# Preparation of a graph kernel: root steps between statistics, index rows cast as they land, spare tile tables ahead of the index transposes

## What is computed

```python
def _layernorm(x, axis=-1, eps=1e-05):
    m = jnp.mean(x, axis=axis, keepdims=True)
    v = jnp.var(x, axis=axis, keepdims=True)
    return (x - m) / jnp.sqrt(v + eps)
...
def _gin_agg(h, src, dst, eps, n_nodes):
    agg = jax.ops.segment_sum(h[src], dst, num_segments=n_nodes)
    return (1.0 + eps) * h + agg
...
x = x + _L0_gnn_ref(_layernorm(x, axis=-1), edge_index, ...)
x = x + _L0_ffn_ref(_layernorm(x, axis=-1)[None], ...)[0]
x = x + _L1_gnn_ref(_layernorm(x, axis=-1), edge_index, ...)
x = x + _L1_ffn_ref(_layernorm(x, axis=-1)[None], ...)[0]
```

## Time and profile before

| | |
|---|---|
| median of three runs | 4575.36 us |
| the profiled execution's own time | 4574.74 us |
| its span | 4572.8 us |
| busy: PE, DVE, ACT, POOL | 3460.2, 1387.5, 491.6, 2855.9 us |
| mean granted TensorE clock | 0.868 of full |

### The profile page before, as it was taken

One profiled execution on the slowest core, in us unless ns is written; L12 is line 12 of the kernel. 1 busy time (PEld: TensorE's weight loads), 2 busy tenths in 40 slices (PEclk: granted clock), 3 DMA queues, 4 the chain that ended last, 5 costly groups with the idle time before them and its releaser, 6 DMA issues. The chain is left out here.

```text
span 4572.8 us, 39338 instructions
## 1 busy us (share of the span) xinstructions
PE 3460.2 (76%) x12646; PEld 2289.5 (50%) x12648; DVE 1387.5 (30%) x3920; ACT 491.6 (11%) x1148; POOL 2855.9 (62%) x2814
## 2 busy tenths in 40 slices
PE   3478777877888898989999976566556656648996
PEld 2345444544553444444544545345444444437986
DVE  5111111211121343334333435233333333442221
ACT  4000000100110000000000002000000000003332
POOL 3666666666646676767767502676666767635664
PEclk7789888988999999999999978777777777779998
DMA  5333333433349666666666527334334333327887
GB/s 184 95 108 112 109 112 110 127 111 111 110 122 329 189 189 197 195 187 194 199 196 206 169 90 236 115 115 119 119 113 129 115 112 115 118 64 187 205 209 188
DMA packets 321328, 687.01 MB, mean 150 GB/s; under 512 B 58976, under 2 KB 148300, under 8 KB 320854
## 3 DMA queue, kind: packets, MB, share of 16 engines
q0 software_dynamic: 169712, 474.01, 37.7%
q10 hardware_dynamic: 86448, 110.35, 7.3%
q1 hardware_dynamic: 64970, 100.14, 6.7%
HBM read 592.43 MB, written 99.13 MB: 151 GB/s over the span
## 5 line engine op out<-in xcount | busy, mean ns | idle before, releaser
L275 POOL DMA_INDIRECT s_edge_rows<-table,w_src_idx x2538 | 2558.2, 1008 | 1207.3 <-issue 714.4
L314 PE MATMUL s_psA<-s_edge_rows,s_onehot 128*128 128x257 f32 (+2 forms) x5076 | 1731.7, 483 | 282.7 <-issue 131.1
L314 PEld LDWEIGHTS s_psA<-s_edge_rows,s_onehot 128*128 128x128 f32 x5076 | 1026.7, 207 | 843.4 <-issue 733.0
L289 DVE TENSOR_TENSOR s_onehot<-w_iota_row,w_dst_l 128x384 f32<-128x384 bf16 x846 | 432.2, 552 | 17.3 <-PEq L144 15.5
L324 PE MATMUL s_psA<-s_edge_rows,s_early 128*128 128x257 f32 (+2 forms) x792 | 263.6, 457 | 11.4 <-issue 9.5
L1943 POOL DMA_INDIRECT acc_rows<-s_y,s_tnode x105 | 166.4, 1585 | 128.1 <-DVE s_y L2063 99.8
L968 PE MATMUL s_psM<-s_h1T,s_w1b 128*128 128x512 f32 (+2 forms) x448 | 196.5, 584 | 53.8 <-ACT s_h1T L870 44.6
L974 PE MATMUL s_psM<-s_w2a,s_hT 128*128 128x512 f32 x392 | 198.2, 651 | 31.8 <-ACT s_hT L874 17.8
L2086 PE MATMUL s_psU<-s_xT,s_w 128*128 128x128 f32 x1680 | 208.3, 278 | 0.0
L2086 PEld LDWEIGHTS s_psU<-s_xT,s_w 128*128 128x128 f32 x1680 | 199.3, 195 | 0.1
L2096 PE MATMUL s_psD<-moe_w,s_hT 128*128 x840 | 199.3, 380 | 0.0
(11 more groups left out here) (352 smaller groups left out, 2771.9 us busy)
## 6 DMA issues: line engine op xcount, KB each, us to landing
s_w<-in_L_ffn_W_dram SPq DMA_DIRECT2D x105, 512.0 KB
s_edge_rows<-table,w_src_idx POOLq DMA_INDIRECT x2538
s_swT<-swt_rows SPq DMA_DIRECT2D x12, 1024.0 KB
table<-s_trow ACTq DMA_DIRECT2D x11, 1024.0 KB
own_rows<-s_own ACTq DMA_DIRECT2D x11, 1024.0 KB
s_self_h<-own_rows ACTq DMA_DIRECT2D x11, 1024.0 KB
swt_rows<-s_swT ACTq DMA_DIRECT2D x11, 1024.0 KB
extra_rows<-w_zeros SPq DMA_DIRECT2D x7, 896.0 KB
```

The costliest lines, as they stand in the source:

```text
L275: pool.indirect_dma_start(self.rows[:, g % self.SLOTS, t, :], None, self.table, bass.IndirectOffsetOnAxis(ap=src_idx[:, at:at + 1], axis=0 ...
L289: return nc.vector.tensor_tensor(into, iota_row[:, q * P:(q + 1) * P].unsqueeze(1).to_broadcast([P, n, P]), dst_l[:, at:at + n].unsqueeze( ...
L314: last = nc.tensor.matmul(banks[b % 2][:, 0:w], self.onehot[:, g % self.AHEAD, t, :], self.rows[:, g % self.SLOTS, t, col:col + w], start= ...
```

## The change

- `BATCH` has six batches instead of four: superblocks 0 to 2, 3 and 4, 5 and 6, 7 and 8, 9 and 10, 11 and 12.
- `scales` is replaced by `scale_step(i, k)`, one of the 16 instructions. Steps of batch i are issued one by one between the `bn_stats` and `bn_aggr` instructions of the two superblocks that follow the batch, eight steps in each. Each step waits for the step before by a semaphore of their own (`s_norm`, 16 counts a batch), no longer at once by `ch.link`. The batch of 9 and 10 has superblock 11 and the single block of 12, and its last six steps follow without cover; the 16 steps of the last batch have no cover but `drow_f`, which stands after the fifth.
- `stats` no longer waits for its last `bn_aggr`; the first step of a batch waits for that.
- `tile_starts` comes after superblock 3 instead of 1, `spare_tiles` after 4 (3), `spare_offsets` after 6 (4), `spare_blocks` after 7 (6). The two casts and `block_base` of `spare_blocks` move to the front of VectorE's program.
- The source rows become floats on GpSimd, behind its gathers, instead of on ScalarE behind its normalising. The two casts have a semaphore each, and the target transposes no longer wait for the source rows.
- On TensorE the slice weights come ahead of the spare tile matmuls, and the sums over `passed` ahead of the index transposes. The transposes wait until VectorE has read the sums out of `psT` (`s_tables`); VectorE reads them behind the last root step. The copies to `src_idx` are now its last work.

```diff
-            BATCH = ((0, 4), (4, 7), (7, 10), (10, SB + 1))
+            BATCH = ((0, 3), (3, 5), (5, 7), (7, 9), (9, 11), (11, SB + 1))
+            TURNS = 16
...
+                pool.wait_ge(s_srow, 16 * GB)
+                pool.tensor_copy(srow_f[:, :, :], srow[:, :, :]).then_inc(s_srowf, 1)
...
+                v.tensor_copy(iota_row[:, :], col_i[:, :])
+                v.tensor_copy(spare[:, :], spare_i[:, :])
+                v.tensor_scalar(block_base[:, :], edge[:, 0:NB], -1.0, -float(CENTRE), ALU.mult, ALU.add)
...
+                def scale_step(i, k):
+                    at = slice(BATCH[i][0] * 4, min(BATCH[i][1] * 4, NB))
+                    o, x, y = rstd[:, at], var[:, at], tmp[:, at]
+                    if k:
+                        dve.wait_ge(s_norm, TURNS * i + k)
+                    if k == 0:
+                        dve.wait_ge(s_dve, aggregated[i])
+                        last = v.tensor_scalar(x, mv[:, at, 1], LN_EPS, None, ALU.add)
...
+                    last.then_inc(s_norm, 1)
...
-                    for q in range(blocks_of(sb).start, blocks_of(sb).stop):
+                    batch = [i for i, (_, end) in enumerate(BATCH) if end in (sb, sb - 1)]
+                    turn = 8 * (sb - BATCH[batch[0]][1]) if batch else 0
+                    for j, q in enumerate(range(blocks_of(sb).start, blocks_of(sb).stop)):
                         last = v.bn_stats(stat[:, q, :], xl[:, q, 0:D])
+                        if batch:
+                            scale_step(batch[0], turn + j)
                     ch.link(last)
...
-                after = {0: (), 1: (first_edges, tile_starts), 3: (spare_tiles,), 4: (spare_offsets,), 6: (spare_blocks,)}
+                after = {1: (first_edges,), 3: (tile_starts,), 4: (spare_tiles,), 6: (spare_offsets,), 7: (spare_blocks,)}
...
+                for k in range(5):
+                    scale_step(len(BATCH) - 1, k)
                 dve.wait_ge(s_drow, 16 * GB)
-                v.tensor_tensor(drow_f[:, :, :], drow[:, :, :], base[:, :].unsqueeze(2).to_broadcast([GR, GB, P]), ALU.subtract).then_inc(s_rowf, 1)
+                v.tensor_tensor(drow_f[:, :, :], drow[:, :, :], base[:, :].unsqueeze(2).to_broadcast([GR, GB, P]), ALU.subtract).then_inc(s_drowf, 1)
+                for k in range(5, TURNS):
+                    scale_step(len(BATCH) - 1, k)
+                spare_tables()
+                dve.wait_ge(s_sw, 1)
+                v.tensor_tensor(slice_b[:, :], slice_b[:, :], psW[2][:, :], ALU.add)
                 dve.wait_ge(s_tr, 2)
                 v.tensor_copy(src_idx[:, 0:PERBANK * GR], psT[2][:, 0:PERBANK * GR])
-                v.tensor_copy(src_idx[:, PERBANK * GR:COLS], psT[3][:, 0:COLS - PERBANK * GR]).then_inc(s_trc, 1)
-                dve.wait_ge(s_sw, 1)
-                v.tensor_tensor(slice_b[:, :], slice_b[:, :], psW[2][:, :], ALU.add)
-                spare_tables()
+                v.tensor_copy(src_idx[:, PERBANK * GR:COLS], psT[3][:, 0:COLS - PERBANK * GR])
...
-                act.wait_ge(s_srow, 16 * GB)
-                ac.activation(srow_f[:, :, :], srow[:, :, :], ACT.Copy).then_inc(s_rowf, 1)
                 act.wait_ge(s_tr, 1)
...
-                pe.wait_ge(s_rowf, 2)
-                edge_transposes(drow_f, psT[0:2])
-                edge_transposes(srow_f, psT[2:4])
...
                 pe.wait_ge(s_passed, 1)
-                pe.wait_ge(s_trc, 2)
                 for h in range(2):
...
                 last.then_inc(s_over, 1)
+                pe.wait_ge(s_tables, 1)
+                pe.wait_ge(s_drowf, 1)
+                edge_transposes(drow_f, psT[0:2])
+                pe.wait_ge(s_srowf, 1)
+                edge_transposes(srow_f, psT[2:4])
```

More of the change, by code:

```diff
@@ L599, in _ @@
                 v.reciprocal(rtemp[:, :], rtemp[:, :]).then_inc(s_rt, 1)
+                def scale_step(i, k):
[6 more added lines that the diff above has]
+                        last = v.tensor_scalar(x, mv[:, at, 1], LN_EPS, None, ALU.add)
+                    elif k == 1:
+                        last = v.tensor_scalar(y.bitcast(I32), x.bitcast(I32), 1, None, ALU.arith_shift_right)
+                    elif k == 2:
+                        last = v.tensor_scalar(o.bitcast(I32), y.bitcast(I32), -1.0, float(0x5F3759DF), ALU.mult, ALU.add)
+                    elif k == TURNS - 1:
+                        last = v.scalar_tensor_tensor(shift[:, at], mv[:, at, 0], -1.0, o, ALU.mult, ALU.mult)
+                    elif k % 4 == 3:
+                        last = v.tensor_tensor(y, o, o, ALU.mult)
+                    elif k % 4 == 0:
+                        last = v.tensor_tensor(y, y, x, ALU.mult)
+                    elif k % 4 == 1:
+                        last = v.tensor_scalar(y, y, -0.5, 1.5, ALU.mult, ALU.add)
+                    else:
+                        last = v.tensor_tensor(o, o, y, ALU.mult)
+                    last.then_inc(s_norm, 1)
@@ L605, in stats @@
                     ch.link(last)
-                    for q in range(blocks_of(sb).start, blocks_of(sb).stop):
+                    for j, q in enumerate(range(blocks_of(sb).start, blocks_of(sb).stop)):
                         last = v.bn_aggr(mv[:, q, :], stat[:, q, :])
[L608 to L614, removed]
+                        if batch:
+                            scale_step(batch[0], turn + size_of(sb) + j)
@@ L616, in first_edges @@
+                    last.then_inc(s_dve, 1)
+                    ch.n += 1
+                    for i, (_, end) in enumerate(BATCH):
+                        if sb + 1 == end:
+                            aggregated[i] = ch.n
+                    if batch and turn:
+                        for k in range(turn + 2 * size_of(sb), TURNS):
+                            scale_step(batch[0], k)
                 def first_edges():
@@ L650, in spare_blocks @@
                     dve.wait_ge(s_fs, 1)
-                    v.tensor_copy(iota_row[:, :], col_i[:, :])
-                    ch.link(v.tensor_copy(spare[:, :], spare_i[:, :]))
-                    v.tensor_scalar(block_base[:, :], edge[:, 0:NB], -1.0, -float(CENTRE), ALU.mult, ALU.add)
                     v.tensor_tensor(step[0:NS, :], psC[0:NS, 29:30], passing[0:NS, 1:2], ALU.subtract)
@@ L760, in _ @@
                 last.then_inc(s_st, 1)
-                pe.wait_ge(s_k, 1)
-                mm(psC[0:NS + 1, 21:22], tri[0:NS, 0:NS + 1], extra[0:NS, :], start=True, stop=True)
-                mm(psC[0:1, 24:25], extra[0:NS, :], ones[0:NS, 0:1], start=True, stop=True).then_inc(s_c, 1)
-                pe.wait_ge(s_f, 1)
-                mm(psC[0:NS + 1, 28:30], shifted[0:NS + 1, 0:NS + 1], passing[:, :], start=True, stop=True).then_inc(s_fs, 1)
                 pe.wait_ge(s_bd, 1)
@@ L773, in _ @@
                 last.then_inc(s_sw, 1)
-                pe.wait_ge(s_rowf, 2)
-                edge_transposes(drow_f, psT[0:2])
-                edge_transposes(srow_f, psT[2:4])
+                pe.wait_ge(s_k, 1)
+                mm(psC[0:NS + 1, 21:22], tri[0:NS, 0:NS + 1], extra[0:NS, :], start=True, stop=True)
+                mm(psC[0:1, 24:25], extra[0:NS, :], ones[0:NS, 0:1], start=True, stop=True).then_inc(s_c, 1)
+                pe.wait_ge(s_f, 1)
+                mm(psC[0:NS + 1, 28:30], shifted[0:NS + 1, 0:NS + 1], passing[:, :], start=True, stop=True).then_inc(s_fs, 1)
                 pe.wait_ge(s_passed, 1)
-                pe.wait_ge(s_trc, 2)
                 for h in range(2):
```

20 lines of the change are left out of this document (10 added, 10 removed).

## The result

| | before | changed |
|---|---|---|
| median of 8 runs | 4573.85 us (4567.25 to 4582.31) | 4558.42 us (4552.49 to 4568.56) |
| ratio | | 0.997, 95% interval 0.996 to 0.9981 |
| the profiled execution | 4574.74 us | 4568.56 us |
| its span | 4572.8 us | 4566.4 us |
| first gather of the next stage | 86.52 us | 72.81 us |

The changed kernel is 0.3% faster, by 15.4 us between the medians. The forecast was 4552, with a range of 4547 to 4563, so the time lies in the range, but the gain is two thirds of the 23.5 us forecast. The profiled execution of the changed kernel happens to be the slowest of its eight, 10.1 us above their median, so I read the gain of the stage from the first gather and not from the span. (The span fell by only 6.4 us, while the first gather came 13.7 us sooner.)

A forecast was written before the change was run, and what follows sets the result against it. GpSimd's gathers pace later stages, so only the preparation's end, set by VectorE, ScalarE and a TensorE-VectorE chain, counts. VectorE's end moves from 84.44 to 59.4, 25.0 less 1.5 for the port: 23.5 off, 4552 us, range 4547 to 4563.

The forecast's parts named there:

- The bound and the passing on: Preparation stage: VectorE, ScalarE, then a TensorE-VectorE chain set its end; each microsecond saved there comes off the total.
- a gain not passed on: Rival: the next stage starts sooner but something else holds it, so the time stays at 4575 us; chance 0.05.
- The start, the superblock and the tail: VectorE: superblock 4 starts at 24.0 us, a superblock with steps takes 2.5, the last stretch shrinks from 13.6 to 6.6.
- the steps hide nothing: Rival: root steps between statistics cost their full 0.20 us, superblocks 3.4 instead of 2.5; 7 us more, 4559; chance 0.10.
- the slow cast: Rival: GpSimd's cast of the source rows delays transposes, copies and barrier; 4596 us if it takes 50; chance 0.05.
- Port: VectorE's steps and compare beside gathers, and GpSimd's cast, cost 1.5 us in all, between 0 and 3.
- SP: SP's stores, behind ScalarE's scaling, have landed at 59.3 us, level with VectorE's end at 59.4.
- The step that failed: VectorE's last root moves from 65.28 to 52.8 us, 12.5 less, 4.6 of it idle time before the cast.
- the stall stays: Rival: VectorE's 4.56 us standstill belongs to the moment, not the cast, and stays; 4556.5 us; chance 0.17.
- The stall moves to the compare: Rival: VectorE's compare cannot start beside row gathers, waiting from 36.6 to 44.0; 7.4 us more, 4559.5; chance 0.10.

The follow-up runs named there:

- the second chip: Unedited kernel before, profiled again on the chip of the second batch, timed in rounds beside the changed kernel: median 4535.17 us, the changed kernel 4517.31.
- the chip without a stall: Chip of the first batch, where the unedited changed kernel had 0.2 us of VectorE idle time between 32 and 45 us: 4155.05 us, kernel before 4181.08.
- late gathers: Changed kernel with GpSimd's 14 row gathers held until the third batch of roots is done: 4161.03 us in the first batch, 4519.39 in the third.

## Why the prediction was right, and where it was wrong

*The bound and the passing on* were right. The first gather came 13.7 us sooner, and the medians fell by 15.4 (interval 8.7 to 18.3). The rival of a gain not passed on is out; that each microsecond is passed on exactly is shown only within such an interval.

*The start, the superblock and the tail* were right. The first scaled block came at 26.33 (forecast 27), a superblock with steps took 2.4 us (49.72 to 52.13; forecast 2.5, so "the steps hide nothing", 3.4, is out), and the tail took 6.6. The rival of the slow cast is out at 0.93 us, against the 1 us taken from the IOTA. TensorE's sums ended at 53.1 and not before 45, but VectorE first read them at 62.76, so this cost nothing.

*Port.* I had 1.5 us, and the name was a guess: no run shows whether VectorE and GpSimd share anything, only how long VectorE's instructions took beside GpSimd's. While GpSimd's cast ran from 45.14 to 46.07, VectorE's L624 took 0.90 instead of 0.15 (as at 47.63) and ended at 46.09; that costs some 0.75. Beside a gather a step was now and then lengthened to 0.38, up to the gather's end (L618, from 28.95 to 29.33; the gather from 28.40 to 29.35), at a price of 0.2 each. The term was about right, and it isn't the stall: the stalled instructions were short ones that had not started.

*SP* was level with VectorE in the forecast. It was ready a little later, 3.5 us lie between VectorE's end and the first gather instead of 2.08 before, and that loss of 1.4 us is the one besides the stall:

```profile
SPq L377 <- DMA table<-x_xl: 3.9, 1, 3.9
```

*The step that failed* is the part of the sum that let the last root go from 65.28 to 52.8 and counted "4.6 the idle time before the cast" among the gains. I took the stall for the cast's. It isn't: it stays when the cast is gone, it struck a root step for 2.5 us and the cast for 0.8 in the kernel before on the second chip, and it strikes instructions that wait on a semaphore in that stretch. The rival "the stall stays" had this, with a chance of 0.17, but its price was wrong too: it let the stall stay at 4.6 us, one wait, one payment. The old order had few waits between 34 and 44 us, the new one has a wait at every second instruction, and it paid 10.1. Put in: 52.8 plus 10.1 is 62.9, and the last root was at 62.68. VectorE's forecast end of 59.4 plus the 2.08 before gives a first gather at 61.5. It came at 72.81, so the miss is 11.3 us, 9.9 of it at the last root and 1.4 SP's.

That the median still lies in the range is in part luck. The first gather missed its own 61 to 64 us by 9, more than the 6.4 by which the median missed 4552, because the medians moved by 1.7 us more than the first gather did and the kernel before ran 1.5 us below the median that I started from. The time of the rival "the stall stays", 4556.5, is 1.9 us off. Those of two false rivals, 4559 and 4559.5, are nearer to 4558.42, so the time alone would have picked a wrong cause.

"The stall moves to the compare" is out. In the changed kernel the compare L691 came at 46.68, after the gathers, and says nothing. But on the chip without a stall it ran at 36.28 for 0.70 us, beside the gathers, with no idle time before it, and so did the old kernel's on the second chip (40.95, shown above).

*What stays open* is the mechanism: why an instruction that waits for a semaphore of VectorE starts late in this stretch, up to 4.6 us on VectorE itself and up to 1.9 on ScalarE, on three of four chips and not on the fourth, and why the waits end on a grid of about 0.7 us.

*A version that may be better.* With late gathers, the first gather of the next stage came 3.3 us before the changed kernel's on the chip with the stall, but 5.2 us after it on the chip without. The total, 4519.39 against 4524.00, is one run each and tells nothing. A gather start between the two was not tried.

## What to carry to other kernels

An idle time that the order of the program doesn't explain belongs to no instruction until it has been moved. Before counting its removal as a gain, price the case that it belongs to the stretch, and then multiply: by the number of waits that the new order puts there. Interleaving short dependent steps with other work saves time where waits are cheap (0.2 us a step became 0.1 here), but each step brings a wait on a semaphore, and where those are dear, a chain laid there pays at many of its links (10.1 us in six pieces here). A stage's model can be checked apart from such a disturbance on a chip that doesn't have it: one run on another chip can show that the disturbance doesn't belong to the kernel alone. And a total inside the forecast range doesn't confirm the parts; here the stage missed by 11 us.

## What was not expected of the hardware

- VectorE's waits on its own semaphores took up to 4.6 us instead of some hundredths, between 32 and 45 us. This was so on three chips in every profiled run of six versions of the program, and in none of four runs on a fourth chip. Holding the row gathers back took it away in the one run on such a chip; taking the stores away did not, though the DMA engines then moved 58 GB/s instead of 262.
- These waits ended on a grid of about 0.7 us, and ScalarE's wait for VectorE on the same grid (1.25 to 1.9 us late instead of 0.04).
- The same kernel took 4574, 4535 and 4543 us on the three chips with the stall, and 4181 on the one without. The mean granted clock was 0.87 and 0.93. VectorE's idle time between 32 and 45 us was 5.6 and 4.3 us in this kernel's two profiles with the stall, a small part of that difference of 350 to 390.
